# Experts of a language-model tower: the third mixture of steps 8 to 18 moved from VectorE to GpSimd, with its weights copied out of PSUM by ScalarE

## Chip, core and metric

One core of a Trainium2 chip. The metric is the device time of one execution in microseconds (us), median of several runs. Engines are named TensorE (PE in the profile), VectorE (DVE), ScalarE (ACT), GpSimd (POOL) and SyncE (SP).

## What is computed

4096 tokens are looked up in a quantized embedding (`h`), go through a 12-head causal attention with a layernorm ahead, and then through a layer of routed experts. The change touches the experts alone. For each of 8 spaces `s` there are 64 experts of 32 hidden units, of which the 4 best are mixed:

```python
z = jnp.einsum('nd,sdr->nsr', xf, P)              # xf: layernorm of h
scores = jnp.einsum('nsr,smr->nsm', z, C)
topv, topi = jax.lax.top_k(scores, K)             # K = 4 of 64
w = jax.nn.softmax(topv, axis=-1)
h = gelu(einsum(z, W1[s, topi]) + b1[s, topi])
yl = einsum(h, W2[s, topi]) + b2[s, topi]
comb = jnp.einsum('nskr,nsk->nsr', yl, w)
out = gelu(comb @ G1 + g1b) @ G2 + g2b
```

The result is added to `h`. The kernel does not gather: it computes the hidden units of all experts for all tokens and multiplies them by a weight that is zero for experts that were not chosen.

## The kernel before

`stage_experts` works on 8 groups of 512 tokens, called group 0 to 7 here. A group has 32 steps (0 to 31). A step handles four tiles of 128 hidden units by 512 tokens, numbered q = 0 to 3, and does for them:

- **up** (`up`, L1465): hidden units into PSUM, two pairs of banks (pair 0 is q 0 and 1, pair 1 is q 2 and 3);
- **gelu** (`gelu`, L1633, ScalarE): one instruction a pair, 128 x 1024, PSUM to `hid` in SBUF;
- **spread** (`spread_weights`, L1475, TensorE): the routing weights of the tile, spread over its 128 rows into one bank of a ring of three PSUM banks;
- **mixture** (`mix`, L1791, VectorE): `hw = hid * bank`, 128 x 512, one a tile;
- **down** (`down`, L1483, TensorE): four tiles of `hw` times W2, summed in PSUM bank 7 over the group's steps. It waits for all four mixtures of its step.

Every engine runs its own program in order; semaphores tie them. TensorE's program at step n is: spread(n, 2), down(n-1), spread(n, 3), up(n+1, pair 1) with spread(n+1, 0) and spread(n+1, 1) between and after, up(n+2, pair 0), the bias matmuls of steps 19 and 21, and then the side items of the step. ScalarE's is: gelu(n+1, pair 1), gelu(n+2, pair 0), then the side items' copies, the exponentials at the end of step 17, and the row sums and squares. VectorE's is: the four mixtures of step n with the routing work of the next group between them (32 maxima in steps 8 to 15, the denominators after mixture (16, 0), 32 `match_replace` marks in steps 16 to 21, reciprocals in step 20).

A ring bank is filled again when what read it is done: an item waits for the one three places before it. Side items take a place in the ring too. They prepare later groups: transposes of x (two items) and z (one), by the table `Z_AT`, for the group two ahead; four score items and four transposes of weights, by `PREP_AT`, for the next group; and three output items, by `OUT_AT`, for the group before.

GpSimd does, a group and in this order: `add_input` of the group before (L1375); for the group two ahead `centre` (after all row sums) and `scale` (seven instructions, L1330 to L1336, after all squares); for the next group `below_best` (L1345, 128 x 2048, after VectorE's denominators); `split_z` (L1340); and `make_weights` twice. Groups 6 and 7 have no group two ahead, group 7 has no next one.

Of the kernel before, what the change touches and what calls it, by code (L numbers as in the profile page):

```python
# [15 lines left out]
ALU = mybir.AluOpType  # L16
ACT = mybir.ActivationFunctionType
AX = mybir.AxisListType

P = 128  # L20
# [1095 lines left out]
def stage_experts(nc, f_p, f_c, f_w1, f_b1, f_w2, f_b2, f_g1, f_g1b, f_g2, f_g2b,  # L1116
# [22 lines left out]
    with ExitStack() as own:  # L1139
        def sb(name, shape, dt=F32):  # L1140
            return own.enter_context(nc.sbuf_tensor(name, shape, dt))

        def sem(name):
            return own.enter_context(nc.semaphore(name))
# [21 lines left out]
        rows_marked, rden_ready, kept_step = sem("rows_marked"), sem("rden_ready"), sem("kept_step")  # L1166
        up_done, gelu_done = sem("up_done"), sem("gelu_done")
        spread, mixed, down_done = sem("spread"), sem("mixed"), sem("down_done")
        comb_ready, gh_ready = sem("comb_ready"), sem("gh_ready")
        out_ready, out_stored = sem("out_ready"), sem("out_stored")  # L1170

# [4 lines left out]
            return [(2 * pair + i // 2 + NQ * (i % 2), (jj + NJ // 2 * (i % 2)) % NJ) for i in range(4)]  # L1176

        rawb2 = sb("rawb2", [P, S, 2 * R])
        rawb2r = sb("rawb2r", [P, S, 2 * R])
        x2 = sb("x2", [P, GW])  # L1180
        c = sb("ln_c", [P, GW])
        sq = sb("ln_sq", [P, GW])
        small = sb("ln_small", [P, 5 * GT])
        power = sb("power", [P, GT])
        o = sb("o", [P, GW])
# [11 lines left out]
        wT = sb("wT", [P, 2, S, GTOK], F16)  # L1197
        hid = sb("hid", [P, 2, NQ, GTOK])
        hw = sb("hw", [P, 2, NQ, GTOK])
        comb = sb("comb", [P, GTOK])  # L1200
        gh = sb("gh", [GH + 1, GTOK])
        total, neg_mean, var, rstd, newton = (small[:, GT * i:GT * i + GT] for i in range(5))
        tok = lambda a: a.rearrange("p (n d) -> p n d", d=D)
# [2 lines left out]
        def need(eng, semaphore, value):  # L1206

            if not (isinstance(value, int) and value <= 0):
                eng.wait_ge(semaphore, value)

        Z_AT = {14: (0,), 15: (1,), 17: (2,)}
        PREP_AT = {5: (3,), 7: (4,), 9: (5,), 11: (6,), 23: (7,), 24: (8,), 26: (9,), 27: (10,)}
        OUT_AT = {1: (0,), 2: (1,), 3: (2,)}
        EXP_AT = 17
        BIAS_AT = (19, 21)


# [2 lines left out]
        MARKS = [(n, q) for n in range(16, 22) for q in range(NQ) for _ in range(2 if n in (18, 19) else 1)]  # L1222
        DEN_AT, RECIPROCALS_AT = (16, 0), (20, 0)

        SUM_AT = {4: 0, 5: 1, 6: 2, 7: 3}
        SQUARE_AT = {8: 0, 9: 1, 10: 2, 11: 3}

        def sides(g, n):
            found = [("out", g - 1, k) for k in OUT_AT.get(n, ())] if g else []
# [6 lines left out]
        def after(g, n, k=1):  # L1236
            return divmod(g * NSTEP + n + k, NSTEP)
# [22 lines left out]
        def ring_bank(item):  # L1260
            return psum[FIRST + at[item] % RING]

        def mixes_done(g, n):
            return (g * NSTEP + n + 1) * NQ

        block = own.enter_context(nc.Block())

# [30 lines left out]
        def _(pool):  # L1298
# [23 lines left out]
            def centre(g):  # L1322
                pool.wait_ge(summed, g)
                link(pool.tensor_scalar(neg_mean, total, -1.0 / D, None, ALU.mult))
                pool.sem_inc(mean_ready, 1)
                link(pool.tensor_tensor(tok(c[:, :]), tok(h_all[:, g * GW:(g + 1) * GW]), wide(neg_mean), ALU.add))

            def scale(g):
                pool.wait_ge(squared, g)
                link(pool.tensor_scalar(var, var, 1.0 / D, LNEPS, ALU.mult, ALU.add))  # L1330
                link(pool.tensor_tensor(rstd, var, power[:, :], ALU.pow))
                link(pool.tensor_tensor(newton, rstd, rstd, ALU.mult))
                link(pool.tensor_tensor(newton, newton, var, ALU.mult))
                link(pool.tensor_scalar(newton, newton, -0.5, 1.5, ALU.mult, ALU.add))
                link(pool.tensor_tensor(rstd, rstd, newton, ALU.mult))
                pool.tensor_tensor(tok(x2[:, :]), tok(c[:, :]), wide(rstd), ALU.mult).then_inc(xn_ready, 1)  # L1336
# [6 lines left out]
            def below_best(g):  # L1343
                pool.wait_ge(den_asked, g + 1)
                pool.tensor_tensor(ew[:, :, :], sc[:, :, 0:M],  # L1345
                                   top[:, :, TOPK:TOPK + 1].to_broadcast([P, GT * S, M]), ALU.subtract)\
                    .then_inc(exp_asked, 1)

            def make_weights(g, part):
# [16 lines left out]
                if part == 0:  # L1366
# [3 lines left out]
                pool.tensor_tensor(wsp[:, half, :, 1, :], by_half, wsp[:, half, :, 0, :], ALU.subtract)\  # L1370
                    .then_inc(w_ready, 1)

            def add_input(g):
                pool.wait_ge(out_taken, 2 * g + 2)
                pool.tensor_tensor(o[:, :], o[:, :], h_all[:, g * GW:(g + 1) * GW], ALU.add).then_inc(out_ready, 1)  # L1375
# [8 lines left out]
            for g in range(NG):  # L1384
                if g:
                    add_input(g - 1)
                if g < NG - 2:
                    centre(g + 2)
                    scale(g + 2)
                if g < NG - 1:  # L1390
                    below_best(g + 1)
                if g < NG - 2:
                    split_z(g + 2)
                if g < NG - 1:
                    for part in range(2):
                        make_weights(g + 1, part)
# [3 lines left out]
        def _(pe):  # L1400
            def bank_free(item):
                m = at[item]
                if m >= RING:
                    before = order[m - RING]
                    if before[0] == "w":
                        pe.wait_ge(mixed, (before[1] * NSTEP + before[2]) * NQ + before[3] + 1)
                    elif before in freed_at:
                        pe.wait_ge(side_free, freed_at[before])
                    else:
                        pe.wait_ge(out_taken, before[1] * 2 + before[2])  # L1410
                return ring_bank(item)
# [63 lines left out]
                pe.matmul(bank, select[rows, jr, :], wT[rows, g % 2, s, :], start=True, stop=True).then_inc(spread, 1)  # L1475

            def down(g, n):
                pe.wait_ge(mixed, mixes_done(g, n))
                if n == 0:
                    need(pe, comb_ready, g)  # L1480
                for i in range(4):
                    s, j = work(n)[i]
                    last = pe.matmul(psum[Y][32 * i:32 * i + 32, :], w2[:, s, j, :], hw[:, n % 2, i, :],  # L1483
                                     start=(n == 0), stop=(n == NSTEP - 1))
                last.then_inc(down_done, 1)
# [82 lines left out]
        def _(act):  # L1568
# [6 lines left out]
                act.dma_start(g2[GH:GH + 1, :], f_g2b.rearrange("(a d) -> a d", a=1)).then_inc(rest_in, 16)  # L1575

            def sum_rows(g, t):
                if t == 0 and g > 1:
                    act.wait_ge(xn_ready, g - 1)
                last = act.activation(sq[:, t * D:(t + 1) * D], h_all[:, (g * GT + t) * D:(g * GT + t + 1) * D],  # L1580
                                      ACT.Identity, accum_out=total[:, t:t + 1])
                if t == GT - 1:
                    last.then_inc(summed, 1)

            def square_rows(g, t):
                if t == 0:
                    act.wait_ge(mean_ready, g)
                last = act.activation(sq[:, t * D:(t + 1) * D], h_all[:, (g * GT + t) * D:(g * GT + t + 1) * D],
                                      ACT.Square, bias=neg_mean[:, t:t + 1], accum_out=var[:, t:t + 1])
                if t == GT - 1:  # L1590
                    last.then_inc(squared, 1)
# [36 lines left out]

            def gelu(g, n, pair):
                if g or n > 1:  # L1630
                    act.wait_ge(mixed, (g * NSTEP + n - 2) * NQ + 2 * pair + 2)
                act.wait_ge(up_done, g * (2 * NSTEP) + 2 * n + pair + 1)
                act.activation(hid[:, n % 2, 2 * pair:2 * pair + 2, :],  # L1633
                               banks[:, pair * 1024:(pair + 1) * 1024].rearrange("p (q n) -> p q n", n=GTOK),
                               ACT.Gelu_apprx_tanh).then_inc(gelu_done, 1)

            def take_mixture(g):
                act.wait_ge(down_done, g * NSTEP + NSTEP)
                act.activation(comb[:, :], psum[Y], ACT.Copy).then_inc(comb_ready, 1)
# [41 lines left out]
            for g in range(NG):  # L1681
                for n in range(NSTEP):
                    next1, next2 = after(g, n), after(g, n, 2)
                    if n == 0 and g:
                        take_mixture(g - 1)
                    if next1[0] < NG:
                        gelu(*next1, 1)
                    if next2[0] < NG:
                        gelu(*next2, 0)
                    for item in sides(g, n):  # L1690
                        take(*item)
                    if n == EXP_AT and g < NG - 1:
                        exponentials(g + 1)
                    if n in SUM_AT and g < NG - 2:
                        sum_rows(g + 2, SUM_AT[n])
                    if n in SQUARE_AT and g < NG - 2:
                        square_rows(g + 2, SQUARE_AT[n])
# [5 lines left out]
        def _(dve):  # L1703
# [105 lines left out]
            split_b2()  # L1809
            for g in range(NG):  # L1810
                for n, q in GAPS:
                    mix(g, n, q)
                    if g < NG - 1:
                        choose(g + 1, n, q)

# [66 lines left out]
```

## Time and profile before

| | before |
|---|---|
| median of 3 runs | 2665.2 us (2664.42 to 2665.51) |
| the profiled execution | 2675.88 us |
| its span, first to last instruction | 2674.1 us |
| TensorE busy in the span | 89% |
| VectorE busy | 69% |
| ScalarE busy | 46% |
| GpSimd busy | 46% |
| mean granted TensorE clock | 0.964 |

The experts take the last 820 us of the span. In the stretches of that part between 1900 and 2600 us VectorE is busy for 87 to 91%, TensorE for 91 to 92%, ScalarE for 74 to 77% and GpSimd for 26 to 32%. Times in the trace are us from the first instruction. A group takes 100 to 104 us, the last one 86.

### The profile page before, as it was taken

To read this page: it belongs to the slowest core of one execution; us is meant where nothing else is said; L and a number is where in the kernel's file an instruction comes from. 1 tells how busy PE (TensorE), PEld (TensorE's weight loads), DVE (VectorE), ACT (ScalarE), POOL (GpSimd) and SP (SyncE) were. 2 spreads that over 40 slices of the span, in tenths; PEclk is the share of its full clock that TensorE was granted. 3 is DMA by queue.
4 is the path that set the end of the run, shared out by engine and by line. 5 is a ranking of instruction groups with operands and counts; after the bars stand their busy time and mean duration, and the time that the engine had idled before them with its cause. 6 is when DMAs were issued, how large, how long until landed. Compare 5 with 4: busy or idle time off the path is not lost. (4 is left out here: it accounts for less than half of the span.)

```text
span 2674.1 us, 42236 instructions
## 1 busy us (share of the span) xinstructions
PE 2390.4 (89%) x16000; PEld 1225.1 (46%) x16000; DVE 1856.7 (69%) x3768; ACT 1237.7 (46%) x1752; POOL 1240.0 (46%) x858
## 2 busy tenths in 40 slices
PE   2555899999999999999999999996899898998998
PEld 1222465655555555555555556543333333333332
DVE  4782765656565656565555656687888888888987
ACT  3332133333333333333333333355777787777776
POOL 5000166667575757575757666662413413324120
PEclk9877999999999999999999999996999999999999
DMA  1002000000001000000000001131000000000000
GB/s 49 12 13 64 8 8 1 10 1 9 8 2 33 1 10 1 9 1 9 1 9 1 3 1 20 19 52 55 9 19 21 15 19 21 15 19 9 19 7 7
DMA packets 42940, 39.33 MB, mean 15 GB/s; under 512 B 26865, under 2 KB 35186, under 8 KB 41842
## 3 DMA queue, kind: packets, MB, share of 16 engines
q1 hardware_dynamic: 40608, 31.18, 5.2%
q0 software_dynamic: 1536, 3.15, 0.4%
q8 instruction: 127, 2.08, 0.3%
q10 hardware_dynamic: 594, 2.31, 0.2%
q14 instruction: 75, 0.61, 0.1%
HBM read 26.13 MB, written 10.49 MB: 14 GB/s over the span
## 5 line engine op out<-in xcount | busy, mean ns | idle before, releaser
L663 POOL TENSOR_TENSOR acc<-acc,pT 128x1024 f32<-128x1024 f32 (+3 forms) x412 | 836.8, 2031 | 239.9 <-ACT pT L1062 203.5
L1062 ACT ACTIVATE pT<-banks 128x1024 f32<-128x1024 f32 x480 | 407.2, 896 | 811.9 <-PE banks L736 742.2
L1791 DVE TENSOR_TENSOR hw<-hid,banks 128x512 f32<-128x512 f32 x1024 | 663.3, 680 | 93.1 <-PE banks L1475 67.8
L881 DVE TENSOR_REDUCE part<-banks 128x2 f32<-128x1024 f32 (+3 forms) x432 | 438.2, 1044 | 312.0 <-PE banks L712 310.2
L1633 ACT ACTIVATE hid<-banks 128x1024 f32<-128x1024 f32 x512 | 496.8, 1022 | 188.6 <-PE banks L1465 167.3
L752 PE MATMUL banks<-pT,v 128*64 128x512 f32 (+3 forms) x1920 | 405.3, 543 | 1.1 <-POOL pT L647 1.1
L1475 PE MATMUL banks<-wT,select 64*128 64x512 f16 x1024 | 342.3, 395 | 38.2 <-DVE hw L1791 17.2
L1465 PE MATMUL banks<-zst,w1c 50*128 50x512 f32 x1024 | 306.9, 546 | 22.1 <-ACT hid L1633 22.1
L1483 PE MATMUL banks<-hw,w 128*32 128x512 f32 x2048 | 277.9, 615 | 0.8 <-DVE hw L1791 0.8
L1475 PEld LDWEIGHTS banks<-wT,select 64*128 64x128 f16 x1024 | 93.6, 94 | 393.0 <-DVE hw L1791 332.3
L752 PEld LDWEIGHTS banks<-pT,v 128*64 128x64 f32 x1920 | 116.6, 136 | 203.0 <-issue 180.9
L732 PE MATMUL banks<-zst,ones 64*128 64x512 f32 x960 | 199.6, 411 | 2.9 <-DVE h_all L939 2.7
L647 POOL TENSOR_SCALAR_AFFINE_SELECT pT<-pT 128x256 f32<-128x256 f32 x192 | 81.5, 425 | 244.7 <-ACT pT L1062 244.5
L712 PE MATMUL banks<-w1c 64*128 64x512 f32 (+3 forms) x1440 | 177.5, 375 | 10.6 <-DVE part L881 4.8
L736 PE MATMUL banks<-w1c 64*128 64x512 f32 (+3 forms) x1440 | 182.6, 361 | 0.0
L732 PEld LDWEIGHTS banks<-zst,ones 64*128 64x128 f32 x960 | 90.1, 183 | 197.8 <-issue 131.1
L924 DVE RECIPROCAL total<-total 128x256 f32<-128x256 f32 x96 | 167.6, 1746 | 3.1 <-ACT total L1070 2.7
L1375 POOL TENSOR_TENSOR o<-o,h_all 128x768 f32<-128x768 f32 x8 | 14.5, 1818 | 305.7 <-ACT o L1652 305.7
L712 PEld LDWEIGHTS banks<-w1c 64*128 64x128 f32 x1440 | 123.5, 186 | 50.1 <-ACT pT L1062 15.6
L1465 PEld LDWEIGHTS banks<-zst,w1c 50*128 50x128 f32 x1024 | 131.1, 194 | 28.6 <-ACT hid L1633 24.9
L736 PEld LDWEIGHTS banks<-w1c 64*128 64x128 f32 x1440 | 128.5, 185 | 17.9
L885 DVE CUSTOM_DVE_ANT_0 banks<-banks,mask 128x128 f32<-128x128 f32 x384 | 103.5, 312 | 29.3 <-PE banks L712 29.3
(225 smaller groups left out, 3167.3 us busy)
## 6 DMA issues: line engine op xcount, KB each, us to landing
zst<-z_scratch SPq DMA_DIRECT2D x48, 128.0 KB, 4.0
z_scratch<-zp SPq DMA_DIRECT2D x8, 512.0 KB, 2.8
out_h<-o SPq DMA_DIRECT2D x8, 384.0 KB, 2.6
xT_scratch<-xs_hi SPq DMA_DIRECT2D x4, 512.0 KB, 2.7
xt_hi<-xT_scratch SPq DMA_DIRECT2D x2, 1024.0 KB, 5.7
w<-in_L_ffn_W ACTq DMA_DIRECT2D x1, 2048.0 KB, 8.0
xt_hi<-in_L_ffn_W SPq DMA_DIRECT2D x12, 128.0 KB, 4.5
v<-in_L_ffn_W SPq DMA_DIRECT2D x12, 128.0 KB, 4.3
```

What stands on the lines that cost most here:

```text
L663: pool.tensor_tensor(acc[:, G % 2, :, off:CH], acc[:, G % 2, :, off:CH], pT[:, slot, :, 0:w], ALU.add).then_inc(summed, 1)
L712: last = pe.matmul(banks[h][:, 0:w], a[u][head(h), i * P:(i + 1) * P], b[u][head(h), c * CH:c * CH + w], start=(k == 0), stop=(k == 2))
L732: pe.matmul(banks[h][:, 0:w], ones[head(h), :], rows[head(h), u, Q, off:CH], start=True, stop=False)
L736: last = pe.matmul(banks[h][:, 0:w], a[u][head(h), kt * P:(kt + 1) * P], b[u][head(h), t0:t0 + w], start=False, stop=(k == 2))
L752: last = pe.matmul(psum[6 + G % 2][head(h), off:CH], v[:, u, kt, head(h)], pT[:, J % PSLOTS, h, 0:CH - off], start=(kt == 0), stop=(j == L ...
L881: last = dve.tensor_reduce(to[:, :, c:c + 1], both[:, :, 0:whole], AX.X, ALU.max)
L1062: act.activation(pT[:, J % PSLOTS, :, 0:CH - off], both[:, :, 0:CH - off], ACT.Exp, scale=E ** -0.5)\
L1465: last = pe.matmul(psum[i], w1[rows, s % NQ, j * P:(j + 1) * P], zst[rows, g % 2, s % NQ, :], start=True, stop=True)
L1475: pe.matmul(bank, select[rows, jr, :], wT[rows, g % 2, s, :], start=True, stop=True).then_inc(spread, 1)
L1483: last = pe.matmul(psum[Y][32 * i:32 * i + 32, :], w2[:, s, j, :], hw[:, n % 2, i, :], start=(n == 0), stop=(n == NSTEP - 1))
L1633: act.activation(hid[:, n % 2, 2 * pair:2 * pair + 2, :], banks[:, pair * 1024:(pair + 1) * 1024].rearrange("p (q n) -> p q n", n=GTOK), A ...
L1791: dve.tensor_tensor(hw[:, n % 2, q, :], hid[:, n % 2, q, :], ring_bank(("w", g, n, q)), ALU.mult).then_inc(mixed, 1)
```

## The change

Of steps 8 to 18 (`LIFTED`) of every group, the mixture of tile 2 is no longer VectorE's. ScalarE copies the spread weights out of the ring bank into a buffer `lift` (`lift_weights`, two halves used in turn), at the start of step n, ahead of gelu(n+1, pair 1); that copy frees the bank. GpSimd multiplies `hid` by `lift` into `hw` (`mix_lifted`). down(n) and gelu(n+2, pair 1) wait for that product too. The 11 multiplications of a group stand in GpSimd's program at fixed places: 8 to 10 between `centre` and `scale`, 11 to 15 after `scale`, 16 to 18 after `below_best`.

The row sums move from steps 4 to 7 to steps 0, 3, 4 and 5, the squares from 8 to 11 to 6 to 9, the x transposes and z from steps 14, 15, 17 to 13, 14, 15. Sums and squares write their unused elementwise results into `x2` in place of a buffer of their own, and `rawb2r` becomes a view of `comb`.

```diff
-        sq = sb("ln_sq", [P, GW])
+        lift = sb("lift", [P, 2, GTOK])
-        Z_AT = {14: (0,), 15: (1,), 17: (2,)}
+        Z_AT = {13: (0,), 14: (1,), 15: (2,)}
+        LIFTED = range(8, 19)
-        SUM_AT = {4: 0, 5: 1, 6: 2, 7: 3}
-        SQUARE_AT = {8: 0, 9: 1, 10: 2, 11: 3}
+        SUM_AT = {0: 0, 3: 1, 4: 2, 5: 3}
+        SQUARE_AT = {6: 0, 7: 1, 8: 2, 9: 3}
...
+            def mix_lifted(g, n):
+                k = lifts(g, n) - 1
+                pool.wait_ge(down_done, g * NSTEP + n - 1)
+                pool.wait_ge(gelu_done, g * (2 * NSTEP) + 2 * n + 2)
+                pool.wait_ge(lifted, k + 1)
+                pool.tensor_tensor(hw[:, n % 2, 2, :], hid[:, n % 2, 2, :], lift[:, k % 2, :], ALU.mult)\
+                    .then_inc(lift_mixed, 1)
...
                 if g < NG - 2:
                     centre(g + 2)
+                for n in LIFTED[:3]:
+                    mix_lifted(g, n)
+                if g < NG - 2:
                     scale(g + 2)
+                for n in LIFTED[3:8]:
+                    mix_lifted(g, n)
                 if g < NG - 1:
                     below_best(g + 1)
+                for n in LIFTED[8:]:
+                    mix_lifted(g, n)
...
                     if before[0] == "w":
-                        pe.wait_ge(mixed, (before[1] * NSTEP + before[2]) * NQ + before[3] + 1)
+                        if is_lifted(before[2], before[3]):
+                            pe.wait_ge(lifted, lifts(before[1], before[2]))
+                        else:
+                            pe.wait_ge(mixed, mixes(*before[1:]))
...
             def down(g, n):
-                pe.wait_ge(mixed, mixes_done(g, n))
+                wait_mixed(pe, g, n, NQ - 1)
...
             def gelu(g, n, pair):
                 if g or n > 1:
-                    act.wait_ge(mixed, (g * NSTEP + n - 2) * NQ + 2 * pair + 2)
+                    wait_mixed(act, *after(g, n, -2), 2 * pair + 1)
...
+            def lift_weights(g, n):
+                k = lifts(g, n) - 1
+                act.wait_ge(spread, g * (NQ * NSTEP) + NQ * n + 3)
+                if k >= 2:
+                    act.wait_ge(lift_mixed, k - 1)
+                act.activation(lift[:, k % 2, :], ring_bank(("w", g, n, 2)), ACT.Copy).then_inc(lifted, 1)
...
+                    if n in LIFTED:
+                        lift_weights(g, n)
                     if next1[0] < NG:
                         gelu(*next1, 1)
...
-                    mix(g, n, q)
+                    if not is_lifted(n, q):
+                        mix(g, n, q)
```

`wait_mixed` waits for VectorE's count and, where tile 2 is lifted and tile 2 or 3 is asked for, for GpSimd's (`lift_mixed`) as well.

On ScalarE, from the last score copy of a group to the table load of the exponentials. Before (`sc` is a score copy, `ln_sq` with `ln_small` a row sum or square, `x2t` an x copy, `zp` and `zc` the two z copies, `den` and `ew` the exponentials):

```order
L1612 ACTIVATE sc<-banks 128x2x4x64
L1588 ACTIVATE ln_sq,ln_small<-h_all,ln_small 128x192
L1633 ACTIVATE hid<-banks 128x1024 x6
L1599 ACTIVATE x2t_hi<-banks 128x512
L1633 ACTIVATE hid<-banks 128x1024 x2
L1599 ACTIVATE x2t_lo<-banks 64x512
L1633 ACTIVATE hid<-banks 128x1024 x4
L1606 ACTIVATE zp<-banks 128x512
L1607 ACTIVATE zc<-banks 128x512
L1619 ACT_TABLE_LOAD
```

Now, from the x copy of step 14 on (`lift` is the new copy):

```order
L1635 ACTIVATE x2t_lo<-banks 64x512
L1678 ACTIVATE lift<-banks 128x512
L1669 ACTIVATE hid<-banks 128x1024 x2
L1642 ACTIVATE zp<-banks 128x512
L1643 ACTIVATE zc<-banks 128x512
L1678 ACTIVATE lift<-banks 128x512
L1669 ACTIVATE hid<-banks 128x1024 x2
L1678 ACTIVATE lift<-banks 128x512
L1669 ACTIVATE hid<-banks 128x1024 x2
L1655 ACT_TABLE_LOAD
L1655 ACTIVATE den<-den 128x128
L1656 ACTIVATE ew<-ew 128x2048
```

The z copies no longer stand right ahead of the exponentials, each step's copy stands behind the copies and squares of the step before, and the copy of step 18 follows the exponentials, ahead of the table load and the gelus. On GpSimd, the part of a middle group from `centre` on, before:

```order
L1326 TENSOR_TENSOR ln_c<-h_all,ln_small 128x768
L1330 TENSOR_SCALAR ln_small<-ln_small 128x4
L1331 TENSOR_TENSOR ln_small<-ln_small,power 128x4
L1332 TENSOR_TENSOR ln_small<-ln_small 128x4
L1333 TENSOR_TENSOR ln_small<-ln_small 128x4
L1334 TENSOR_SCALAR ln_small<-ln_small 128x4
L1335 TENSOR_TENSOR ln_small<-ln_small 128x4
L1336 TENSOR_TENSOR x<-ln_c,ln_small 128x768
L1345 TENSOR_TENSOR ew<-sc,top 128x2048
L1340 TENSOR_TENSOR zp<-zc,zp 128x512
```

And now:

```order
L1343 TENSOR_TENSOR ln_c<-h_all,ln_small 128x768
L1395 TENSOR_TENSOR hw<-hid,lift 128x512 x3
L1347 TENSOR_SCALAR ln_small<-ln_small 128x4
L1348 TENSOR_TENSOR ln_small<-ln_small,power 128x4
L1349 TENSOR_TENSOR ln_small<-ln_small 128x4
L1350 TENSOR_TENSOR ln_small<-ln_small 128x4
L1351 TENSOR_SCALAR ln_small<-ln_small 128x4
L1352 TENSOR_TENSOR ln_small<-ln_small 128x4
L1353 TENSOR_TENSOR x<-ln_c,ln_small 128x768
L1395 TENSOR_TENSOR hw<-hid,lift 128x512 x5
L1362 TENSOR_TENSOR ew<-sc,top 128x2048
L1395 TENSOR_TENSOR hw<-hid,lift 128x512 x3
```

Product 11 stands behind the seven instructions of `scale`, and product 16 behind `below_best`. TensorE's program keeps its order but for the three side items that moved.

## Rows read from the trace of the kernel before

**Rows 1.** Timeline, last group, plain steps: start us, us, engine, line, what, count [idle].

```profile
2604.52 1.06 PE L1483 MATMUL banks<-hw,w 128*32 128x512 f32 x8
...
2606.38 1.94 ACT L1633 ACTIVATE hid<-banks 128x1024 f32<-128x1024 f32 x2 [0.61 <-PE banks L1465]
...
2607.07 1.06 PE L1483 MATMUL banks<-hw,w 128*32 128x512 f32 x8
```

**Rows 2.** Timeline, group 2, steps 9 and 10, the loop through TensorE.

```profile
2089.73 0.96 PE L1439 MATMUL banks<-w1c,zst 48*128 48x64 f32 x7
...
2090.78 1.06 PE L1483 MATMUL banks<-hw,w 128*32 128x512 f32 x8
...
2092.27 0.69 DVE L1791 TENSOR_TENSOR hw<-hid,banks 128x512 f32<-128x512 f32 x1 [0.26 <-PE banks L1475]
...
2093.33 1.06 PE L1483 MATMUL banks<-hw,w 128*32 128x512 f32 x8
```

**Rows 3.** Timeline, group 2, VectorE: two mixtures with a maximum between them.

```profile
2099.40 0.67 DVE L1791 TENSOR_TENSOR hw<-hid,banks 128x512 f32<-128x512 f32 x1
...
2100.13 0.67 DVE L1791 TENSOR_TENSOR hw<-hid,banks 128x512 f32<-128x512 f32 x1
```

**Rows 4.** Timeline, group 2, ScalarE: gelus of step 8, then a square.

```profile
2086.44 1.94 ACT L1633 ACTIVATE hid<-banks 128x1024 f32<-128x1024 f32 x2 [0.64 <-PE banks L1465]
...
2088.27 0.46 ACT L1588 ACTIVATE ln_sq<-h_all,ln_small 128x192 f32<-128x192 f32 x1
```

**Rows 5.** Timeline, group 2: step 7's down, ScalarE's side work, z, exponentials.

```profile
2084.58 1.06 PE L1483 MATMUL banks<-hw,w 128*32 128x512 f32 x8
...
2084.86 0.60 ACT L1612 ACTIVATE sc<-banks 128x512 f32<-128x512 f32 x1
2085.33 0.37 ACT L1580 ACTIVATE ln_sq<-h_all 128x192 f32<-128x192 f32 x1
...
2115.15 1.13 PE L1426 MATMUL banks<-x2t_hi,pm_hi 128*128 128x512 f32 x2 [0.17 <-DVE hw L1791]
...
2117.47 1.06 PE L1483 MATMUL banks<-hw,w 128*32 128x512 f32 x8
...
2117.86 0.59 ACT L1607 ACTIVATE zc<-banks 128x512 f32<-128x512 f32 x1
2118.47 1.28 ACT L1619 ACT_TABLE_LOAD   x1
...
2121.89 1.28 ACT L1633 ACT_TABLE_LOAD   x1
```

**Rows 6.** Timeline, group 2: first and last instruction of scale; mixture (15, 3); below_best.

```profile
2098.23 0.20 POOL L1330 TENSOR_SCALAR ln_small<-ln_small 128x4 f32<-128x4 f32 x1 [10.46 <-ACT ln_sq L1588]
...
2100.75 1.47 POOL L1336 TENSOR_TENSOR x<-ln_c,ln_small 128x768 f32<-128x768 f32 x1
...
2107.77 0.69 DVE L1791 TENSOR_TENSOR hw<-hid,banks 128x512 f32<-128x512 f32 x1 [0.27 <-PE banks L1475]
...
2109.60 3.69 POOL L1345 TENSOR_TENSOR ew<-sc,top 128x2048 f32<-128x2048 f32 x1 [7.38 <-DVE den L1759]
...
2118.53 1.29 POOL L1340 TENSOR_TENSOR zp<-zc,zp 128x512 fp32r<-128x512 f32 x1 [5.23 <-ACT zc L1607]
```

**Rows 7.** Groups of GpSimd instructions by line and form: busy us, mean ns | idle.

```profile
L663 POOL TENSOR_TENSOR acc<-acc,pT 128x512 f32<-128x512 f32 x48 | 63.6, 1326 | 3.9
```

**Rows 8.** Line L1340 in the whole trace: ns min/median/max.

```profile
L1340 POOL TENSOR_TENSOR zp<-zc,zp x7: 1283/1292/1663, 1845.3 to 2430.6; 128x512 fp32r<-128x512 f32 x7
```

**Rows 9.** Timeline, group 6: downs of steps 7 and 16, gelus of step 17, exponentials.

```profile
2500.88 1.07 PE L1483 MATMUL banks<-hw,w 128*32 128x512 f32 x8
...
2528.21 1.06 PE L1483 MATMUL banks<-hw,w 128*32 128x512 f32 x8
...
2530.09 1.94 ACT L1633 ACTIVATE hid<-banks 128x1024 f32<-128x1024 f32 x2 [1.24 <-PE banks L1465]
2532.04 1.28 ACT L1619 ACT_TABLE_LOAD   x1
```

More of the change, by code:

```diff
@@ L1168, in stage_experts @@
         spread, mixed, down_done = sem("spread"), sem("mixed"), sem("down_done")
+        lifted, lift_mixed = sem("lifted"), sem("lift_mixed")
         comb_ready, gh_ready = sem("comb_ready"), sem("gh_ready")
@@ L1178, in stage_experts @@
         rawb2 = sb("rawb2", [P, S, 2 * R])
-        rawb2r = sb("rawb2r", [P, S, 2 * R])
         x2 = sb("x2", [P, GW])
         c = sb("ln_c", [P, GW])
-        sq = sb("ln_sq", [P, GW])
         small = sb("ln_small", [P, 5 * GT])
@@ L1199, in stage_experts @@
         hw = sb("hw", [P, 2, NQ, GTOK])
+        lift = sb("lift", [P, 2, GTOK])
         comb = sb("comb", [P, GTOK])
+        rawb2r = comb[:, 0:S * 2 * R].rearrange("p (s r) -> p s r", r=2 * R)
         gh = sb("gh", [GH + 1, GTOK])
@@ L1261, in ring_bank, with is_lifted, lifts, mixes @@
             return psum[FIRST + at[item] % RING]
-        def mixes_done(g, n):
-            return (g * NSTEP + n + 1) * NQ
+        def is_lifted(n, q):
+            return q == 2 and n in LIFTED
+        def lifts(g, n):
+            return g * len(LIFTED) + sum(k in LIFTED for k in range(n + 1))
+        def mixes(g, n, q):
+            return (g * NSTEP + n) * NQ + q + 1 - (lifts(g, n) if q >= 2 else lifts(*divmod(g * NSTEP + n - 1, NSTEP)))
+        def wait_mixed(eng, g, n, q):
+            need(eng, mixed, mixes(g, n, q))
+            if q >= 2 and n in LIFTED:
+                eng.wait_ge(lift_mixed, lifts(g, n))
         block = own.enter_context(nc.Block())
@@ L1579, in sum_rows @@
                     act.wait_ge(xn_ready, g - 1)
-                last = act.activation(sq[:, t * D:(t + 1) * D], h_all[:, (g * GT + t) * D:(g * GT + t + 1) * D],
+                last = act.activation(x2[:, t * D:(t + 1) * D], h_all[:, (g * GT + t) * D:(g * GT + t + 1) * D],
                                       ACT.Identity, accum_out=total[:, t:t + 1])
@@ L1587, in square_rows @@
                     act.wait_ge(mean_ready, g)
-                last = act.activation(sq[:, t * D:(t + 1) * D], h_all[:, (g * GT + t) * D:(g * GT + t + 1) * D],
+                last = act.activation(x2[:, t * D:(t + 1) * D], h_all[:, (g * GT + t) * D:(g * GT + t + 1) * D],
                                       ACT.Square, bias=neg_mean[:, t:t + 1], accum_out=var[:, t:t + 1])
```

## Prediction

> **What bounds the kernel now.** I read the busy time by stretches first, then the timeline of a plain stretch of the last group, then of one whole group. In the expert part no engine is full. What sets a step is a loop, and the plain steps, which have no routing work, show it bare: downs start 2.55 us apart, at 2604.52 and 2607.07 [rows 1]. The loop's parts stand in rows 2: down(9) starts at 2090.78, spread(10, 3) is behind it on TensorE, mixture (10, 3) starts 1.49 later at 2092.27 and ends at 2092.96, and down(10) starts 0.37 after that. Call D(n) the start of down(n) and T(n) the end of mixture (n, 3): T(n+1) = D(n) + 2.18, D(n+1) = T(n+1) + 0.37, so 2.55 a step. A side item of TensorE stands inside the 0.37. A score item starts 0.05 after T, at 2089.73, and the down at 2090.78, 1.10 after T [rows 2], which makes that step 3.28; for an x item I take the same. z starts at 2115.15, so T is 2115.10, and the down follows at 2117.47, 2.37 after T [rows 5]: 4.55.
>
> VectorE limits only steps that have routing work and no side item: with a maximum behind each mixture they start 0.73 apart [rows 3], 2.91 a step. What the change can win on VectorE is therefore 0.36 in each of the four such steps of 8 to 15, and some 0.4 more in the marks of step 17: about 1.9 us in each of seven groups, 13 us.
>
> **What the change adds to the chain.** A lifted step's product has a path of its own, copy on ScalarE, product on GpSimd, and the down waits for it. The copy of step n+1 stands behind the two gelus that ScalarE runs in step n, and the first of those starts 1.86 after D(n-1), at 2606.38 with the down at 2604.52 [rows 1]. The pair occupies ScalarE for 1.84 (2086.44 to 2088.27 [rows 4]). The copy is 128 x 512, the form of zc, 0.59, taken as 0.60; from its end at 2118.45 [rows 5] GpSimd started 0.08 later [rows 6].
>
> The product itself no row shows. Nearest are additions of two full 128 x 512 operands at 1.326 us [rows 7] and the subtraction of z at 1.292 [rows 8]; I take **1.30**, since both operands are full. The ends are 0.98 (two thirds of the 1.47 of a 128 x 768 product with one broadcast operand [rows 6]) and 1.66 (the longest 128 x 512 [rows 8]). With 0.06 to the down, D(n+1) = D(n-1) + 1.86 + 1.84 + 0.60 + 0.08 + 1.30 + 0.06 = D(n-1) + 5.74: **2.87 a step**, more than the loop's 2.55 and hardly less than the 2.91 of the steps it relieves. On VectorE the same multiplication takes about 0.68 in the rows, half as much. The Trainium skill, GPSIMD Engine Reference, section 3.1, has GpSimd at about 2.6 cycles an element for two-input elementwise work and keeps VectorE as the rule for it. From its 1.2 GHz an estimate by that page is 1.11 us; with it the time below would be 2686 and not 2692.
>
> **A middle group (0 to 5), step by step**, from D(7) = 0. Before it is at 2084.58 [rows 5].
>
> - Step 8. ScalarE's score copy starts 0.28 after D(7) and the next instruction 0.48 later (2084.86, 2085.33 [rows 5]); the square takes 0.46 [rows 4], 0.54 with the reading of its sum. Behind them the copy ends at 1.90, the product at 3.28, D(8) = 3.34 against 2.55 by the loop.
> - Step 9, score: loop, 3.34 + 3.28, D(9) = 6.62 (the product is there at 6.22).
> - Step 10: gelus from D(8) + 1.86 to 7.04, score copy to 7.52, square to 8.06, copy to 8.66, product to 10.04. D(10) = 10.10, not 9.17.
> - Step 11: `scale` now stands before product 11. It takes 3.99 (2098.23 to 2102.22 [rows 6]): product 11 runs from 14.13 to 15.43, D(11) = 15.49, where the loop with its score item would give 13.38. **2.1 us of waiting.**
> - Step 12, loop: 18.04. Steps 13 and 14, loop with x: 21.32, 24.60. T(15) = 26.78, and z makes D(15) = 29.15.
> - Step 16: below_best started 1.15 after T(15), the end of the mixture at 2107.77 [rows 6], and takes 3.69. Product 16 stands behind it: 27.93 + 3.69, then 0.05 and 1.30, D(16) = 33.03; the loop gives 31.70.
> - Step 17, loop: 35.58. The exponentials follow the gelus of step 17 directly, z no longer being ahead of them. In group 6, which has no z, those gelus start 1.88 after D(16) and the table load 1.95 later [rows 9]; I use 1.86 and 1.95. So the load is at 33.03 + 3.81 = 36.84. Before it is at 2118.47 - 2084.58 = 33.89 [rows 5]. Moving z out of the way is inside this sum: its 2.0 over a loop step went from step 17 to step 15 and is not saved.
> - After the exponentials the copy of step 18 is ahead of the gelu table load: 0.60 more. Product 18 and down(18) come about 3.4 later, but step 19's third mixture waits for the gelu anyway, so I add nothing.
>
> Sum: 36.84 - 33.89 + 0.60 = **+3.55 a group, 21.3 for six**. Behind step 19 the group runs as before. `make_weights` finishes some 2 us later against TensorE, with over 4 us of slack before the first weights are turned; if that were gone, TensorE would wait in steps 23 to 27. The earlier sums and squares fit in ScalarE's idle 0.6 of a step and cost nothing; without that gap they would delay gelus. The dropped buffers cost nothing. No DMA is added: z's bounce is issued two steps earlier, for a group that is 20 steps away.
>
> **Group 6** has no squares, no `scale` and no z. The same steps give D(8) = 2.80, D(9) 6.08, D(10) 9.02, D(11) 12.30, D(12) 15.24, then chain steps: D(13) 18.04, D(14) 20.98, T(15) 23.16. With below_best D(16) = 29.41, and the load is at 33.22. Before it is at 2532.04 - 2500.88 = 31.16 [rows 9]. With the copy: 2.06 + 0.60 = +2.7. **Group 7** is plain, 11 steps of 2.87 in place of 2.55: +3.5.
>
> All together 21.3 + 2.7 + 3.5 = **+27.5 us**. The rows are of an execution of 2675.88 us, 10.7 above the median of 2665.2; the difference is put on the median: 2692.7, forecast **2692**. The product's time enters four times in a middle group, five in group 6 and 5.5 in group 7, 34.5 in all: with 0.98 the time is 2682, with 1.66 it is 2705. What a measurement can tell from no change is 0.2%, 5.3 us.
>
> **Rivals.**
>
> 1. *VectorE's relief wins: faster.* The place is the copy in steps 8 to 18: if it ran right after its spread, between the gelus, the product would be done before T and only the 1.9 us a group of relief would be left: -13, **2652**. It decides once copy and product end before T(n+1), that is, when 5.74 falls under 5.11 and neither `scale` nor below_best is in the way. For it: ScalarE idles 0.6 us a step and VectorE is the busier engine. Against it: ScalarE's program has the gelus first, and GpSimd's has two long items between products.
> 2. *The chain in the steps hides, the queue waits don't.* Relief -13, `scale` 2.1 x 6 = +13, the copy ahead of the table load 0.6 x 7 = +4: +4, **2669**. For it: where side items stretch a step to 3.28 the chain of 2.87 is hidden by the loop. Against it: group 7 has no side items and four steps of groups 0 to 6 neither.
> 3. *The product is slower beside VectorE*, as the 1.66 us of [rows 8]: 2705. It is the forecast's own upper end.
>
> That the change does not do what it says is excluded by the order of the programs.
>
> **How the numbers follow.** Forecast mechanism, with rival 3 as its end: 0.72, all slower. Rival 1: 0.14, faster. Rival 2: 0.14, of which 0.12 within 0.2% and 0.02 above. Slower 0.74, same 0.12, faster 0.14. The range takes in the ends of the product's time, 2682 to 2705, and rival 2 down to 2663; rival 1 is left out.
>
> **What would show it.** Right: downs in the last group's steps 8 to 18 about 2.87 apart; weight loads of the down released by GpSimd; a gap of over 5 us between down(10) and down(11) in groups 0 to 5 with the products behind `scale`; the table load some 2.9 us later after down(7). Wrong: downs still 2.55 apart in group 7 (the copy is then earlier than I think); `scale` over before product 10's time; a product of under 0.9 us. If VectorE still showed 2.91 a step, it and not the chain would be the bound.

## Result and the profile after

| | before | change |
|---|---|---|
| median of 4 runs | 2665.4 us | 2703.9 us |
| ratio, 95% interval | | 1.0147 (1.0135 to 1.0159) |
| profiled execution / its span | 2675.88 / 2674.1 | 2708.93 / 2706.9 us |
| first to last down of the experts in it | 806.2 us | 845.2 us |

The change is 38.6 us slower; the forecast was 27 slower, 2692, with 2705 as its upper end. The last row of the table is worked out from the trace's down rows. The spans of the two profiled executions differ by less than that (32.8), because the attention ahead of the experts, which is the same, took 5.9 us less in the second. So I compare experts with experts: +39.0. That is one execution of each kernel; two kernels below were profiled twice, and their experts differ by 1.1 and 1.4 us, so differences of a few us are read from the ratios as well.

Busy time of each engine in the change:

```profile
PE 2400.0 (89%) x16000; PEld 1230.5 (45%) x16000; DVE 1808.1 (67%) x3680; ACT 1278.6 (47%) x1840; POOL 1352.3 (50%) x946
```

VectorE was busy for 48.6 us less (88 mixtures are gone), GpSimd for 112.3 more. The product's line over the whole trace, with durations (ns min/median/max), and who waited for it (us, times):

```profile
L1395 POOL TENSOR_TENSOR hw<-hid,lift x88: 1262/1277/1287, 1872.2 to 2659.2; 128x512 f32<-128x512 f32 x88
...
  PE banks L1518: 26.2, 27
```

The product takes 1.28 us and hardly varies; TensorE's matmuls waited for it 27 times, 26.2 us in all. L1518 is the down, L1395 the product, L1510 the spread, L1678 the copy. The timeline of group 1, steps 7 to 11 (it answers to [rows 2] and [rows 6]):

```profile
1978.61 1.07 PE L1518 MATMUL banks<-hw,w 128*32 128x512 f32 x8
1980.57 1.28 POOL L1395 TENSOR_TENSOR hw<-hid,lift 128x512 f32<-128x512 f32 x1 [4.87 <-ACT lift L1678]
...
1982.00 1.06 PE L1518 MATMUL banks<-hw,w 128*32 128x512 f32 x8 [0.77 <-POOL hw L1395]
...
1988.64 0.20 POOL L1347 TENSOR_SCALAR ln_small<-ln_small 128x4 f32<-128x4 f32 x1
...
1988.82 1.07 PE L1518 MATMUL banks<-hw,w 128*32 128x512 f32 x8 [0.81 <-POOL hw L1395]
...
1991.17 1.47 POOL L1353 TENSOR_TENSOR x<-ln_c,ln_small 128x768 f32<-128x768 f32 x1
1992.59 2.50 POOL L1395 TENSOR_TENSOR hw<-hid,lift 128x512 f32<-128x512 f32 x2
...
1994.00 1.07 PE L1518 MATMUL banks<-hw,w 128*32 128x512 f32 x8 [1.64 <-POOL hw L1395]
```

The bracket behind a down is the idle time of TensorE and what ended it. down(8) waited 0.77 us for its product and down(10) 0.81. `scale` began behind product 10 and product 11 behind `scale`, so down(11) came 5.18 after down(10) and TensorE idled for 1.64 of it. In groups 1 and 3 every down of the routing stretch came within 0.15 us of the forecast's sum (us from down(7); change: group 1, before: group 2):

```
step             8     9    10     11     12     13     14     15     16     17
forecast        3.34  6.62  10.10  15.49  18.04  21.32  24.60  29.15  33.03  35.58
change          3.39  6.68  10.21  15.39  17.95  21.31  24.59  29.29  33.10  35.65
before          2.55  6.19   8.75  12.58  15.13  18.05  21.69  25.11  27.70  32.89
```

Down(16) of group 1, behind the product that follows `below_best`:

```profile
2010.29 1.27 POOL L1395 TENSOR_TENSOR hw<-hid,lift 128x512 f32<-128x512 f32 x1
2011.71 1.07 PE L1518 MATMUL banks<-hw,w 128*32 128x512 f32 x8 [1.19 <-DVE hw L1836]
```

It starts 0.15 after the product's end and 1.6 after that of step 16's last mixture (2010.07). So the 1.19 us are a wait for the product; the work of VectorE that the bracket names is a mixture of step 17.

What the forecast did not have is mainly in groups 0, 2, 4 and 5. Behind the wait of step 11 the granted clock fell there. Stretches of group 2 (us: busy us of PE, PEld, DVE, ACT, POOL; granted clock, DMA):

```profile
2097.00:2102.00 5.00, 3.22 (x28) 1.69 (x24) 2.51 (x9) 3.41 (x5) 4.59 (x8) 0.94 0.00 0
2102.00:2107.00 5.00, 5.00 (x24) 1.33 (x23) 2.42 (x7) 1.86 (x3) 0.96 (x1) 0.50 0.00 0
2107.00:2112.00 5.00, 4.80 (x31) 1.92 (x27) 2.77 (x9) 3.49 (x6) 1.40 (x2) 0.88 0.00 0
```

down(11) is at 2101.88, behind 1.62 us of idle TensorE, and is followed by 5 us at a granted clock of 0.50: 1.2 GHz in place of 2.4. Downs and the matmuls around them take about twice as long:

```profile
2101.88 1.93 PE L1518 MATMUL banks<-hw,w 128*32 128x512 f32 x8 [1.62 <-POOL hw L1395]
...
2105.80 1.94 PE L1518 MATMUL banks<-hw,w 128*32 128x512 f32 x8
...
2110.16 1.07 PE L1518 MATMUL banks<-hw,w 128*32 128x512 f32 x8
```

down(13) is 23.66 behind down(7) there, against 21.31 in group 1: 2.4 us. Groups 0, 4 and 5 lost 1.0, 1.3 and 2.4. Group 6 has no `scale`, but product 16 stands behind `below_best` with no z ahead of it to fill the wait. There TensorE idled for 2.78 us, and the clock fell as well; in the kernel before it was whole at that place:

```profile
2554.03 1.06 PE L1518 MATMUL banks<-hw,w 128*32 128x512 f32 x8 [2.78 <-POOL hw L1395]
...
2556.82 1.93 PE L1518 MATMUL banks<-hw,w 128*32 128x512 f32 x8
```

Counted over the experts, from the granted clock in the traces, TensorE ran at half clock for 40 us before and for 74 in the change.

The exponentials of group 1 (it answers to the end of [rows 5]):

```profile
2015.55 1.28 ACT L1655 ACT_TABLE_LOAD   x1
...
2018.86 0.58 ACT L1678 ACTIVATE lift<-banks 128x512 f32<-128x512 f32 x1
2019.45 1.28 ACT L1669 ACT_TABLE_LOAD   x1
2019.49 0.61 PE L1510 MATMUL banks<-wT,select 64*128 64x512 f16 x1 [3.26 <-ACT lift L1678]
...
2019.60 1.27 POOL L1395 TENSOR_TENSOR hw<-hid,lift 128x512 f32<-128x512 f32 x1 [5.95 <-ACT lift L1678]
...
2020.74 1.94 ACT L1669 ACTIVATE hid<-banks 128x1024 f32<-128x1024 f32 x2
...
2021.02 1.94 PE L1518 MATMUL banks<-hw,w 128*32 128x512 f32 x8 [0.29 <-DVE hw L1836]
```

The load is 36.94 after down(7), 36.84 in the sum. The copy delays the gelus as expected. TensorE, which needs the copied bank, idles 3.26 us for it and comes back at half clock. That much is hardly new: before, it idled 2.85 us there for the gelu, also with half clock behind it (0.50 from 2124.6 to 2127.6, group 2). New is that down(18), which came ahead of the exponentials before, is now behind them and takes 1.94 us at that clock.

### The profile page after: what moved, and what is told of

Its sections match the earlier page's. It is cut to its first block and busy times, and to the rows that moved or that the text cites. A ratio compares the mean times of both kernels' runs of the same rounds, so it can differ in the third digit from the quotient of the medians.

```text
span 2706.9 us, 42498 instructions
## 1 busy us (share of the span) xinstructions
PE 2400.0 (89%) x16000; PEld 1230.5 (45%) x16000; DVE 1808.1 (67%) x3680; ACT 1278.6 (47%) x1840; POOL 1352.3 (50%) x946
## 5 line engine op out<-in xcount | busy, mean ns | idle before, releaser
L1836 DVE TENSOR_TENSOR hw<-hid,banks 128x512 f32<-128x512 f32 x936 | 605.1, 681 | 180.3 <-PE banks L1510 167.0
L1510 PE MATMUL banks<-wT,select 64*128 64x512 f16 x1024 | 348.2, 402 | 52.5 <-ACT lift L1678 24.1
L1518 PE MATMUL banks<-hw,w 128*32 128x512 f32 x2048 | 285.6, 630 | 38.2 <-POOL hw L1395 26.2
L1500 PE MATMUL banks<-zst,w1c 50*128 50x512 f32 x1024 | 315.6, 564 | 3.8 <-ACT hid L1669 3.8
L1510 PEld LDWEIGHTS banks<-wT,select 64*128 64x128 f16 x1024 | 95.3, 95 | 412.3 <-DVE hw L1836 275.4
L1395 POOL TENSOR_TENSOR hw<-hid,lift 128x512 f32<-128x512 f32 x88 | 111.9, 1276 | 204.9 <-ACT lift L1678 201.0
```

The costliest lines, as they stand in the source:

```text
L1500: last = pe.matmul(psum[i], w1[rows, s % NQ, j * P:(j + 1) * P], zst[rows, g % 2, s % NQ, :], start=True, stop=True)
L1836: dve.tensor_tensor(hw[:, n % 2, q, :], hid[:, n % 2, q, :], ring_bank(("w", g, n, q)), ALU.mult).then_inc(mixed, 1)
```

## Experiments

In all of them the ratio is to the kernel before, run on the same chip; "experts" is first to last down in the one profiled execution, 806.2 us before and 845.2 in the change (ratio 1.0147). The edits are to the changed kernel.

**The moves alone.**

```diff
-        LIFTED = range(8, 19)
+        LIFTED = ()
```

> No mixture is lifted; only the earlier row sums, squares, x items and z remain of the change. Waits theory (the loss comes from downs that wait for the copy and product of tile 2): -3 us against before, about 2662, since z costs the same 2 us of loop in step 15 as in step 17 and ScalarE has room for sums and squares. Rival, the moves themselves cost (z and x in steps that VectorE fills with maxima): +5 to +15.

Measured 0.9973 (0.9961 to 0.9985), experts 798.3: faster by 8, more than the 3 expected. The moved items cost 1.5 us up to down(16) (29.17 behind down(7) in place of 27.70), step 17 without z gives 2.0 back (down(17) 32.36 in place of 32.89), and the exponentials' table load, no longer behind z's copies, is at 33.00 and not 33.89. That is 5 us in six groups. The rest lies in steps 18 to 20, where TensorE was at half clock for less time in this execution (27 us over the experts, 40 before; 37 when the same kernel was run again below). The rival that the moves cost something falls. The lifting itself therefore costs 47 us of experts' time, not 39.

**Step 11 not lifted.** `LIFTED` is a list without 11; GpSimd has products 8 to 10, `scale`, 12 to 15, `below_best`, 16 to 18.

```diff
-        LIFTED = range(8, 19)
+        LIFTED = (8, 9, 10, 12, 13, 14, 15, 16, 17, 18)
```

> Step 11 is not lifted, so no product stands right behind scale on GpSimd. Waits theory: the 2 us gap between down(10) and down(11) goes in six groups, -10 us; and the half-clock stretches behind that gap, seen in four of six groups of the change and worth 1.0 to 2.4 us each, go too, -7: about 2687. Rival, a cost spread evenly over the 88 lifted products (0.44 us each, from a slower GpSimd or ScalarE): -3.5, about 2700, with the gap or the half clock elsewhere.

Measured 1.0103 (1.0088 to 1.0119), experts 830.4: 15 us by the experts, 12 by the ratios, from one of eleven steps; 17 had been expected. Stretches of group 2, where step 11 lies in the first:

```profile
2103.00:2108.00 5.00, 4.66 (x35) 2.09 (x36) 3.58 (x12) 3.38 (x5) 3.51 (x8) 1.00 0.00 0
2108.00:2113.00 5.00, 4.32 (x32) 1.79 (x33) 4.35 (x13) 3.97 (x5) 2.55 (x2) 1.00 0.01 2
```

down(11) follows down(10) by 3.50, not 5.18, the clock stays whole, and down(13) is 19.88 behind down(7) in all six groups: neither the wait nor any of the four half-clock stretches behind it is left (in group 5 the clock fell once behind down(16) instead, worth 1.2 us at down(17)). An even cost for each product (3.5 us) falls.

**The copy between the gelus**, all steps lifted:

```diff
-                    if n in LIFTED:
-                        lift_weights(g, n)
                     if next1[0] < NG:
                         gelu(*next1, 1)
+                        if next1[1] in LIFTED:
+                            lift_weights(*next1)
```

> The copy of step n+1 runs on ScalarE between gelu(n+1, pair 1) and gelu(n+2, pair 0), no longer behind both gelus, the side copies and the exponentials. All 11 steps stay lifted. Waits theory: downs of the last group 2.55 apart again (2.99 on average in the change); steps 8 and 10 lose their 0.8 and 0.9; step 18's product is done before the exponentials end. scale (now about 1.7 us of wait) and below_best (1.3) stay: about +7 against before, 2672. Rival, even cost a product: 2704, unchanged.

Measured 1.0131 (1.0116 to 1.0147), experts 842.9: my number was wrong by 28 us. In group 7, which has no side items, it did what was expected: downs 2.55 apart in all but one step, 0.4 lost in eleven steps where the change loses 4.9. Elsewhere the copy stands in the way of the rest of ScalarE. Timeline, group 2, around down(7) and down(8):

```profile
2096.78 1.07 PE L1518 MATMUL banks<-hw,w 128*32 128x512 f32 x8
2096.88 0.60 ACT L1678 ACTIVATE lift<-banks 128x512 f32<-128x512 f32 x1 [0.63 <-PE banks L1510]
2097.38 1.02 ACT L1669 ACTIVATE hid<-banks 128x1024 f32<-128x1024 f32 x1
...
2098.28 0.60 ACT L1648 ACTIVATE sc<-banks 128x512 f32<-128x512 f32 x1
...
2098.94 0.39 PE L1510 MATMUL banks<-wT,select 64*128 64x512 f16 x1 [0.67 <-ACT sc L1648]
...
2099.82 1.06 PE L1518 MATMUL banks<-hw,w 128*32 128x512 f32 x8
```

The spread that the copy needs stands behind the score item on TensorE, so ScalarE idles 0.63 for it, the score copy starts 1.50 after the down in place of 0.28 [rows 5], and the spread that needs the score copy's ring bank waits for it in turn. down(8) is 3.05 behind down(7), not 2.55. The product of this step is early now and nothing waits for it; its copy is what others wait for. Product 11, still behind `scale`, is waited for as before (down(11) idles 1.19 us ahead of it, and the clock fell behind that in groups 1 to 4).

**The same without steps 11 and 16.** `LIFTED = (8, 9, 10, 12, 13, 14, 15, 17, 18)` with the order of the last run.

> Copy between the gelus, and steps 11 and 16 not lifted, so that no product stands right behind a long item of GpSimd. Waits theory: only VectorE's relief (0.36 us in steps 9, 13, 14 and about 0.4 in 17) and the earlier exponentials are left: faster than before by about 9 us, 2656 (2650 to 2662). Rival, even cost a product: 72 of 88 products, +31, 2696.

Measured 1.0071 (1.0057 to 1.0085), experts 827.2. Better than the last by 16 with the long items out of the way, but still 21 over before, where 9 under had been expected. The copies in steps with side items remain, and I had allowed nothing for them. In group 3, against the run with the moves alone, steps 8, 10, 12, 14 and 15, whose copies run in steps with a score or x item, are longer by 0.50, 0.54, 0.52, 0.69 and 0.83 us; steps 9, 13, 17 and 18, whose copies run in steps without one, are shorter by 0.2, 0.1, 0.6 and 0.6. In groups 1, 4 and 6 the clock also fell behind down(7) (0.50 from 1988.2 to 1991.5 in group 1), behind an idle time of 0.67 us for the score copy, and down(9) came 1.4 us later than in the others.

**Step 18 not lifted.** `LIFTED = range(8, 18)`.

> The change with step 18 not lifted: no copy between the exponentials and the gelu table load, and down(18) waits for VectorE alone. Waits theory: 0.6 us of ScalarE and the 1.1 us by which down(18), pushed behind the exponentials and into a half-clock stretch, lengthens step 18 go in seven groups, -12 against the change, +27 against before (ratio about 1.010). Rival, even cost a product (0.44 us): -3.5, ratio about 1.013.

Measured 1.0116 (1.0101 to 1.0132), experts 836.8, 8.4 under the change. By the ratios that is between the two numbers expected, so this run alone does not decide between them; the trace does. In the two groups without a fallen clock behind step 11, down(19) comes 45.7 after down(7) and not 47.9, but down(20) 49.2 against 50.5: part of the gain is given back in step 20.

**Steps 11, 16 and 18 not lifted.** The copy is where the change has it.

> The change with steps 11, 16 and 18 not lifted, the copy where the change has it. Waits theory: on top of the run without step 11, D(16) comes 1.3 us earlier in six groups and 2.5 in group 6, and step 18 gives 1.7 in seven: -22 against that run, about +4 against before (ratio 1.001 to 1.004). Rival, even cost: 64 products, +28, ratio 1.010.

Measured 1.0028 (1.0019 to 1.0037), experts 811.2. Of the 47 us that lifting costs, three of eleven steps hold 34: those whose product stands behind `scale`, behind `below_best` and behind the exponentials. The other eight steps a group hold 13, and 4 of these are in group 7, where no side item hides the chain.

**x and z back in steps 14, 15 and 17.**

```diff
-        Z_AT = {13: (0,), 14: (1,), 15: (2,)}
+        Z_AT = {14: (0,), 15: (1,), 17: (2,)}
```

> The change with x and z back in steps 14, 15 and 17. Waits theory: below_best is no longer covered by z's matmuls in step 15 and ScalarE waits for z ahead of the exponentials again: the exponentials start about 1 us later in six groups, +6 against the change, ratio about 1.017. Rival, where z stands is indifferent: as the change, 1.0145.

Measured 1.0227 (1.0212 to 1.0243), experts 867.0: +22 against the change, not +6. Timeline, group 2, steps 16 and 17:

```profile
2127.88 1.06 PE L1518 MATMUL banks<-hw,w 128*32 128x512 f32 x8 [2.34 <-POOL hw L1395]
...
2130.36 2.07 PE L1461 MATMUL banks<-x2t_hi,pm_hi 128*128 128x512 f32 x2
...
2132.37 2.07 PE L1462 MATMUL banks<-x2t_lo,pm_lo 64*128 64x512 f32 x2
...
2134.80 1.93 PE L1518 MATMUL banks<-hw,w 128*32 128x512 f32 x8
```

At full clock my sum was nearly right: in group 0, where the clock had not fallen yet, down(16) is at 32.97 behind down(7), and a z step of 4.55 and 1.0 to the load make 38.5, 1.6 us later than the 36.9 of the change and not 1, or 9 to 10 us in six groups. The clock did the rest. Without z in step 15 TensorE waits 2.34 us for the product behind `below_best`, and the clock falls behind that in all six groups, in the change in none of them. z runs in the half-clock stretch, 2.07 us an instruction pair in place of 1.13 [rows 5]; over the experts TensorE was at half clock for 113 us and not 74. In the change z's own matmuls cover half of that wait, and 1.19 us are left.

**Three steps, copy between the gelus.** From what was left, a version: lift only where VectorE held the step up (9, 11, 13), with the copies in steps 8, 10 and 12 that have no side item, and product 11 ahead of `scale`.

```diff
-        LIFTED = range(8, 19)
+        LIFTED = (9, 11, 13)
...
-                for n in LIFTED[:3]:
+                for n in LIFTED[:2]:
                     mix_lifted(g, n)
```

The products behind `scale` and behind `below_best` are cut to match, and the order on ScalarE is that of the copy between the gelus.

> Only steps 9, 11 and 13 lifted, the copy between the gelus of the step before (8, 10 and 12 have no side item, so spread and ScalarE are free), product 11 ahead of scale. Theory: each lifted step gives back what VectorE held it up by when nothing was lifted (0.36, 0.55, 0.36 us), 1.3 us in each of seven groups: -9 against the run with the moves alone, ratio to before about 0.994. Rival, ScalarE or GpSimd is the cost wherever a copy stands: no gain over the moves alone, 0.997 or more.

Measured 0.9960 (0.9947 to 0.9974), experts 793.6: below both kernels, but 5 us under the moves alone where 9 had been expected, and on another chip than they, with ratios whose intervals overlap (0.9961 to 0.9985 for the moves). So it was run once more on one chip with the moves alone, and with the copy put back behind the gelus:

> The moves alone once more, on the same chip as the next two, for a comparison with them: ratio to before 0.997, down(16) 29.17 us behind down(7) in the middle groups.

> Steps 9, 11 and 13 lifted, copy between the gelus, once more beside the moves alone: 5 to 8 us under them (ratio to before 0.994 to 0.996), down(16) about 28.1 behind down(7). Rival, no gain from lifting at all: equal to the moves alone within 0.1%.

> The same three steps, with the copy where the change puts it, behind both gelus and the side work of the step before. Waits theory: the copy of step 9 comes behind a square, product 9 ends about 6.3 us after down(7) where the loop gives 5.8: 0.5 us a group lost, steps 11 and 13 about even; ratio 0.996 to 0.998, half to all of the gain over the moves alone gone. Rival, the place of the copy does not matter with so few of them: as the run before this one.

| | median, us | ratio to before | experts, us | down(9), down(16) after down(7), group 2 |
|---|---|---|---|---|
| moves alone | 2662.2 | 0.9968 (0.9958 to 0.9978) | 799.7 | 6.19, 29.17 |
| three steps, copy between | 2655.3 | 0.9942 (0.9929 to 0.9954) | 792.5 | 5.83, 28.08 |
| three steps, copy behind | 2665.3 | 0.9976 (0.9965 to 0.9986) | 796.8 | 6.31, 28.64 |

Three steps with the copy between are 7 us under the moves alone, and the intervals don't touch. Down(16) comes 1.1 us earlier in five groups and 0.7 in groups 0 and 1, 6.9 in all, which is the whole gain. Expected had been 1.3 a group: step 11 gives 0.36 and not 0.55. Timeline of the middle row, steps 7 to 9 of group 2:

```profile
2074.58 1.07 PE L1518 MATMUL banks<-hw,w 128*32 128x512 f32 x8
...
2077.13 1.07 PE L1518 MATMUL banks<-hw,w 128*32 128x512 f32 x8
2077.37 0.59 ACT L1678 ACTIVATE lift<-banks 128x512 f32<-128x512 f32 x1
2077.85 1.03 ACT L1669 ACTIVATE hid<-banks 128x1024 f32<-128x1024 f32 x1
2078.13 1.28 POOL L1395 TENSOR_TENSOR hw<-hid,lift 128x512 f32<-128x512 f32 x1 [6.46 <-ACT lift L1678]
...
2080.41 1.07 PE L1518 MATMUL banks<-hw,w 128*32 128x512 f32 x8
```

The product ends at 2079.41, a microsecond before its down, which comes 3.28 after the last, the loop's own time with a score item. With the copy behind, down(9) is at 6.31, as the sum for that order said (6.3), and the gain at down(16) is 0.5 us a group and not 1.1. The expectation left out group 7, where VectorE holds nothing up: there the three lifted steps cost 2.4 us with the copy behind (down(9) at 5.88 in place of 5.11) and nothing with the copy between. The gain over the moves in the experts is 3 us, and in the medians none can be shown: the intervals overlap, and the executions of both kernels spread over 10 us.

## Why the prediction was right, and what its size missed

Point by point, by the forecast's steps:

- **The loop** (2.55 a step, 3.28 with a score or x item, 4.55 with z) held: it gave down(12) to down(15) and down(17) of groups 1 and 3 within 0.15 us. The x item, taken as long as a score item, was. Steps 21 to 31 are as long as before in these groups, as forecast.
- **The product's time**, 1.30 between 0.98 and 1.66: it took 1.277, 0.02 less. The row nearest in kind, two full operands, was the right one; 1.66 never appeared beside VectorE's work. The estimate of 1.11 us by the 2.6 cycles an element of the Trainium skill, GPSIMD Engine Reference, section 3.1, was too short by 0.17.
- **The chain through copy and product.** In group 7 two steps take 5.90, not 5.74: the handing over from ScalarE to GpSimd took 0.17 and from GpSimd to TensorE 0.15, where 0.08 and 0.06 had been taken. The downs are not evenly 2.87 apart, the sign that the forecast named, but mostly 3.35 and 2.55 in turn, 3.00 on average. With step 8 at 3.39 the group lost 4.9, forecast 3.5.
- **scale** (2.1 expected): down(11) 5.18 behind down(10). Shown by the run without step 11.
- **below_best**, D(16) = 33.03: 33.10, behind 1.19 us of idle TensorE. That z in step 15 covers half of the wait was in the sum only through T(15); the run with z back was 22 us slower.
- **The exponentials**: load 36.84 forecast, 36.94 measured; gelus +3.5.
- **The term that was too small** is "loop" behind step 11, which took TensorE's clock as given. The wait of 1.6 us is not paid once: in four of six groups the matmuls behind it ran at half clock, 7 us in the profiled execution. Of the 39.0, groups 0 to 5 have 29.0, where 21.3 were forecast, and this is nearly all of the difference.
- **"so I add nothing" for down(18)** was the second. It runs at half clock behind the exponentials, down(19) came 4.6 later than before and not 3.55; step 20 gave about 1 of it back, and groups 1 and 3 ended at +3.8 and +3.9, 0.4 of the latter ahead of its down(7). Group 6 has 5.1 against 2.7: down(17) is at 32.81, where the sum had 31.96 (0.6 of it chain steps again, 0.2 the clock that fell behind down(16)), and the rest is behind the exponentials, where the clock is at half for 6.8 us in this group too and was not before.
- **The sums, squares and moved items cost nothing**: right, and more: alone they gain 8 us.
- **"VectorE limits only steps that have routing work and no side item"** was read wrongly: before, step 9 takes 3.64 and step 11 takes 3.83, with a score item each, and not the loop's 3.28. The sum for the change did not need it, the worth of VectorE's relief did.

That 2703.9 lies inside the range, 1 us under its end, is partly luck. The end of 2705 stood for a product of 1.66 us, and the product took 1.28; what brought the time there was the clock and the longer hand-overs.

Rival 1 (VectorE's relief wins) is wrong for eleven steps; for three it is right in kind, with 7 us in place of 13. Its condition, copy and product early and neither `scale` nor `below_best` in the way, was met in the run with the copy between the gelus and without steps 11 and 16: no down waits for a product there. It was 21 us slower than before. What it missed is that ScalarE's 0.6 us idle a step is no place for the copy where a side item delays the spread that the copy reads. Rival 2 is excluded by the run without steps 11, 16 and 18: there the queue waits are gone and what the other eight cost, 13 us against the moves alone, does not hide.

Left open: what decides whether the clock falls in a given group. Behind down(11) it fell in four of six groups in the change, without step 18 and with the copy between the gelus, and in five of six with z back; in the runs in which product 11 did not stand behind `scale` it fell there in none. So the wait brings it about, but not each time. How much of the 39 us is the clock in all is open too: the 34 us more at half clock can have cost up to 17. Open is also step 20's length, which differs by up to 1.3 us between groups of one run already before.

## What to carry to other kernels

Before work is moved to an idle engine, look where it lands in that engine's program: a 1.3 us product is cheap until it stands behind a 4 us item that nobody waited for. The wait itself may not be all: here 1.6 us of it on TensorE cost up to 2.4 more, at half clock. Take the shortest loop of the steady state, add the detour to it, and lift only the steps that the relieved engine sets, with the copy at a place where its input is already there. Three steps lifted in this way gained 7 us over none; eleven had lost 47, and even the eight steps whose products wait for no long item lost 13.

## What the runs showed of the hardware

- TensorE idle for 1.6 us (down(11) of group 2) was followed by 5 us at a granted clock of 0.50. The clock fell at four of six like places of the change; the other two stayed at full clock. Behind the longer waits for product 16, 2.34 us in the run with z back and 2.78 in group 6 of the change, it fell at every place. The Trainium skill, TensorE: Matmul & The Clock Gate, Part 1, describes the throttled clock as the state that activity releases, which agrees with where these stretches lie, behind the waits.
- The f32 product of 128 x 512 on GpSimd took 1.262 to 1.287 us in all 88 places, with VectorE busy for 74% of that time; two such products in a row ran in 2.50.
- A load of ScalarE's table took 1.28 us, each way, ahead of the exponentials and ahead of the gelus (2015.55 and 2019.45 in group 1).
